# A language-model layer on one Trainium2 core: router logits of seven batches are taken during the next batch's attention, and the router's and first expert's inputs are loaded there

## The reference

```python
h = h + attention(layernorm(h))     # 8 heads of 128, rotary positions, causal softmax
h = h + experts(layernorm(h))
```

```python
scores = jax.nn.softmax(xt @ Wr, axis=-1)        # Wr is 256 by 8
G, idx = jax.lax.top_k(scores.T, k)              # each expert takes its 1024 best tokens
X_in = xt[idx]
h = jax.nn.gelu(jnp.einsum('ekd,edh->ekh', X_in, W1) + b1[:, None, :], approximate=False)
X_e = jnp.einsum('ekh,ehd->ekd', h, W2) + b2[:, None, :]
out = jnp.zeros((N, D)).at[idx.reshape(-1)].add((G[..., None] * X_e).reshape(E * k, D))
```

## Time and profile before

| what | value |
|---|---|
| median of 3 runs | 1323.09 us (1321.56 to 1324.31) |
| span of the profiled execution | 1321.1 us |
| TensorE busy | 1156.3 us, 88% of the span |
| DVE busy | 913.1 us, 69% |
| POOL busy | 746.2 us, 56% |
| ACT busy | 609.6 us, 46% |
| attention ends (start of the last `evacuate`, L402) | 774.27 us |
| first TensorE instruction of the experts' block | 807.52 us |
| first gathered rows on TensorE | 887.7 us |

### The profile page before, as it was taken

How to read it: one execution, slowest core, us unless ns; L and a number is a source line. 1 busy time by engine, 2 the same in 40 slices (tenths; PEclk the granted TensorE clock), 3 DMA queues, 4 the chain that set the end, 5 groups by cost and what they waited for, 6 DMA issues and landing times. The chain is left out here.

```text
span 1321.1 us, 22367 instructions
## 1 busy us (share of the span) xinstructions
PE 1156.3 (88%) x7255; PEld 990.9 (75%) x7255; DVE 913.1 (69%) x1980; ACT 609.6 (46%) x1306; POOL 746.2 (56%) x783
## 2 busy tenths in 40 slices
PE   2899999999999999999999983018999989898995
PEld 2688887878878878878888851017989879897995
DVE  4788888898898988888888844855545444454532
ACT  3454545545545555545455532005455445453542
POOL 2676676776776766766766610032473474644735
PEclk9999999999999999999999997559999999898998
DMA  5000100100100100101000003020351442423322
GB/s 179 1 17 1 37 30 0 40 24 0 40 24 27 33 4 32 32 0 36 28 1 32 17 32 105 0 97 17 96 126 23 110 113 30 114 36 92 54 29 33
DMA packets 42165, 57.51 MB, mean 44 GB/s; under 512 B 8896, under 2 KB 34944, under 8 KB 41984
## 3 DMA queue, kind: packets, MB, share of 16 engines
q0 software_dynamic: 13824, 21.24, 8.7%
q1 hardware_dynamic: 28288, 35.58, 8.0%
HBM read 35.71 MB, written 16.91 MB: 40 GB/s over the span
## 5 line engine op out<-in xcount | busy, mean ns | idle before, releaser
L1131 DVE TENSOR_TENSOR hT_lo<-hid,hT_hi 128x512 fp32r<-128x512 f32 x128 | 89.5, 702 | 160.9 <-ACT hT_hi L1245 160.9
L268 ACT ACTIVATE prob<-bank,row_min 128x512 f32<-128x512 f32 (+3 forms) x256 | 136.1, 532 | 112.6 <-DVE row_min L389 112.5
L199 POOL TENSOR_SCALAR prob<-prob,row_inv 128x512 f32<-128x512 f32 (+3 forms) x256 | 135.3, 540 | 68.3 <-DVE row_inv L393 66.8
L954 POOL DMA_INDIRECT got<-routed_rows,tokens x64 | 91.3, 1426 | 139.2 <-DVE tokens L1125 122.1
L1243 ACT ACTIVATE hid<-up,b_e 128x512 f32<-128x512 f32 x128 | 88.1, 688 | 161.3 <-PE up L1310 156.4
L339 DVE TENSOR_TENSOR pT_lo<-bank,pT_hi 128x384 fp32r<-128x384 f32 (+1 forms) x192 | 114.4, 596 | 50.5 <-ACT pT_hi L248 50.4
L212 POOL TENSOR_TENSOR kT_lo<-k_cos,kT_hi 128x512 fp32r<-128x512 f32 x64 | 82.6, 1290 | 77.7 <-ACT kT_hi L248 77.7
L248 ACT ACTIVATE oT_hi<-bank 128x512 fp32r<-128x512 f32 x64 | 38.3, 599 | 185.2 <-PE bank L519 177.3
L206 POOL TENSOR_TENSOR q_cos<-q_cos,q_sin 128x512 f32<-128x512 f32 x64 | 82.4, 1288 | 55.0 <-DVE q_sin L376 54.8
L974 POOL DMA_INDIRECT out<-y,tokens x64 | 103.0, 1609 | 17.3 <-issue 14.8
L389 DVE TENSOR_REDUCE row_min<-bank 128x1 f32<-128x512 f32 (+3 forms) x256 | 112.6, 481 | 0.2
(11 more groups left out here) (196 smaller groups left out, 3873.4 us busy)
## 6 DMA issues: line engine op xcount, KB each, us to landing
raw<-in_w SPq DMA_DIRECT2D x16, 1024.0 KB, 8.5
emb_res<-emb SPq DMA_DIRECT2D x8, 512.0 KB, 3.7
out<-h SPq DMA_DIRECT2D x8, 512.0 KB, 3.0
routed_rows<-x SPq DMA_DIRECT2D x8, 512.0 KB
x<-in_wq SPq DMA_DIRECT2D x1, 1024.0 KB, 7.5
x<-in_wk SPq DMA_DIRECT2D x1, 1024.0 KB, 11.2
x<-in_wv SPq DMA_DIRECT2D x1, 1024.0 KB, 5.3
x<-in_wo SPq DMA_DIRECT2D x1, 1024.0 KB, 8.5
```

What stands on the lines that cost most here:

```text
L199: nc.gpsimd.tensor_scalar(pr, pr, row_inv[:, h % 2, k:k + 1], 1.0, ALU.mult, ALU.mult).then_inc(s["norm_done"], 1)
L268: nc.scalar.activation(prob[:, h % 2, col:col + w], s_ps[bk][:, pc:pc + w], ACT.Exp, bias=row_min[:, h % 2, k:k + 1], scale=-1.0, accum_ou ...
L954: pool.indirect_dma_start(got[i][:, c, :], None, a["rows"][:, :], bass.IndirectOffsetOnAxis(tokens[i][:, c:c + 1], 0))\
L1131: nc.vector.tensor_tensor(out, in_, hi.bitcast(F32), ALU.subtract)\
```

## The change

- **Logits during attention.** `x2` shrinks to one batch (4 blocks), and a second buffer of that size, `x2T`, holds its transpose. In batches 1 to 7, for the batch before: at the end of slots 5 and 6 TensorE makes four transposes each into `proj_ps[1]` (`x2_turn`), ACT copies each to `x2T` (`x2_copy`), and at the end of slot 7 TensorE takes the logits token by expert into 32 columns of `proj_ps[1]` (`logits`: 8 float32 products, stationary `x2T` 128x128, moving `wr` 128x8), which ACT copies to `logit` (`keep_logits`). `project` of the key waits for these copies in slots 6, 7 and 0.
- **The router stage** handles the last batch alone: one group of 8 transposes, two copies, 8 products. The softmax of the first 28 blocks is taken in DVE's and ACT's gaps there, that of the last 4 at the end. The store of `score_rows` waits for the fourth signal of `r_score`, where it waited for the first.
- **Loads.** `groups_f` and `b1_rows` load at the kernel's start, behind `wr`; the first expert's `raw1` and `raw2` load in the last batch, ahead of the last store of `h2`.
- **What follows from the smaller `x2`.** Query, key and value weights pass through `raw1`, `raw2` and the `x2` pair, the output weight through `prob`, the mask through `k_cos`. `normalise2` waits for the last store of `x2` and its transposes.
- TensorE waits for `wr_in` ahead of its very first instruction, where it waited for it at the router's start. Batch 1 is written out as well; the loop covers batches 2 to 6.

```diff
@@ build_attention, SyncE
             sp.dma_start(wr[:], a["wr"].rearrange("(t p) e -> p t e", p=P))\
                 .then_inc(s["wr_in"], 16)
+            sp.dma_start(early["groups_f"][:], a["groups"][:, :, :]).then_inc(s["c_in"], 16)
+            sp.dma_start(early["b1_rows"][:], a["b1"].rearrange("e (t p) -> (e t) p", p=P))\
+                .then_inc(s["c_in"], 16)
...
             batches(sp, body)
+            sp.dma_start(early["raw1"][:], a["w1"][0].rearrange("(t p) n -> p t n", p=P))\
+                .then_inc(s["raw_in"], 16)
+            sp.dma_start(early["raw2"][:], a["w2"][0].rearrange("(t p) m -> p t m", p=P))\
+                .then_inc(s["raw_in"], 16)
             store_h2(B - 1)
@@ ScalarE
+            def x2_copy(b, kt):
+                after(act, "x2_tr", KT * b + kt + 1)
+                nc.scalar.activation(x2T[:, kt, :], proj_ps[1][:], ACT.Copy)\
+                    .then_inc(s["x2_copied"], 1)
+
+            def keep_logits(b):
+                after(act, "l_done", b + 1)
+                nc.scalar.activation(
+                    logit[:, bass.ds(b * TB, TB), :],
+                    l_ps.rearrange("p (t e) -> p t e", e=E), ACT.Copy).then_inc(s["l_kept"], 1)
...
                     if ok(h - 1):
                         exp(b, h - 1, 3)
+                    if h in (5, 6) and not (isinstance(b, int) and b == 0):
+                        x2_copy(b - 1, h - 5)
+                    if h == 7 and not (isinstance(b, int) and b == 0):
+                        keep_logits(b - 1)
@@ TensorE, project
                 if h == 0:
                     after(pe, "xt_lo", KT * (b + 1))
+                    if x == "k" and not (isinstance(b, int) and b < 2):
+                        after(pe, "l_kept", b - 1)
...
                     after(pe, "k_rope", n)
+                    if h in (6, 7) and not (isinstance(b, int) and b == 0):
+                        after(pe, "x2_copied", KT * (b - 1) + h - 5)
@@ TensorE
+            def x2_turn(b, kt, n):
+                after(pe, "x2_ready", TB * (b + 1))
+                after(pe, "k_rope", n + 1)
+                for tb in range(TB):
+                    last = nc.tensor.transpose(proj_ps[1][:, tb * P:(tb + 1) * P],
+                                               x2[:, tb, kt * P:(kt + 1) * P], ident[:])
+                last.then_inc(s["x2_tr"], 1)
+
+            def logits(b, live_xt):
+                after(pe, "x2_copied", KT * (b + 1))
+                if live_xt:
+                    after(pe, "xt_lo", KT * (b + 3))
+                for tb in range(TB):
+                    for kt in range(KT):
+                        last = nc.tensor.matmul(l_ps[:, tb * E:(tb + 1) * E],
+                                                x2T[:, kt, tb * P:(tb + 1) * P], wr[:, kt, :],
+                                                start=tb == 0 and kt == 0,
+                                                stop=tb == TB - 1 and kt == KT - 1)
+                last.then_inc(s["l_done"], 1)
+
             pe.wait_ge(s["tables_in"], 48)
+            pe.wait_ge(s["wr_in"], 16)
             xt(0)
```

More of the change, by code:

```diff
@@ L92, in build_attention @@
             out_done r_evac
-            stats2_done aggr2_done var2_eps rstd2_done apart""".split()
+            stats2_done aggr2_done var2_eps rstd2_done apart x2_tr x2_copied l_done l_kept""".split()
         s = {n: sem(n) for n in names} | shared
@@ L111, in batches @@
             body(0, range(8), lambda h: h >= 0)
-            with eng.Fori(1, B - 1) as b:
+            body(1, range(8), lambda h: True)
+            with eng.Fori(2, B - 1) as b:
                 body(b, range(8), lambda h: True)
@@ L658, in body @@
                         turn(b, h - 2, 2)
+                    if h in (5, 6) and not (isinstance(b, int) and b == 0):
+                        x2_turn(b - 1, h - 5, n)
+                    if h == 7 and not (isinstance(b, int) and b == 0):
+                        logits(b - 1, len(slots) == H)
             batches(pe, body)
@@ L738, in _ @@
             last.then_inc(s["r_aggr"], 1)
[L739 to L740 removed]
+            below_top(old, logit[:, old, :])
             dve.wait_ge(s["r_rstd"], 1)
+            dve.wait_ge(s["x2_out"], 16 * (B - 1))
             for tb in range(TB):
[L743 removed]
+                nc.vector.tensor_scalar(x2[:, tb, :], h2[:, tb, :], mean_var[:, tb, 0:1],
                                         rstd[:, tb:tb + 1], ALU.subtract, ALU.mult)\
@@ L815, in build_experts @@
-def build_experts(nc, a, ident, score, shared):
+            pe.wait_ge(s["x2_ready"], NB)
+            for kt in range(KT):
+                for tb in range(TB):
+                    last = nc.tensor.transpose(x_ps[kt][:, tb * P:(tb + 1) * P],
+                                               x2[:, tb, kt * P:(kt + 1) * P], ident[:])
+                last.then_inc(s["r_tr"], 1)
+            for kt in range(KT):
+                pe.wait_ge(s[f"r_copy{kt}"], 1)
+            for tb in range(TB):
+                for kt in range(KT):
+                    last = nc.tensor.matmul(l_ps[:, tb, :], x2T[:, kt, tb * P:(tb + 1) * P],
+                                            wr[:, kt, :], start=tb == 0 and kt == 0,
+                                            stop=tb == TB - 1 and kt == KT - 1)
@@ L817, in build_experts @@
+            last.then_inc(s["r_logits_done"], 1)
+def build_experts(nc, a, ident, score, early, shared):
     ctx = ExitStack()
@@ L823, in ps @@
             return ctx.enter_context(nc.psum_tensor(name, list(shape), F32))
-        groups_f, groups = sb("groups_f", [P, 2, P]), sb("groups", [P, 2, P], BF16)
+        groups_f, b1_rows, raw1, raw2 = (early[n] for n in ("groups_f", "b1_rows", "raw1", "raw2"))
+        groups = sb("groups", [P, 2, P], BF16)
         EH = 2
```

177 lines of the change are left out of this document (68 added, 109 removed).

## The result

The changed kernel takes 1330.11 us (median of 8 runs, 1322.88 to 1335.1), the kernel before 1322.74 us beside it (8 runs, 1319.85 to 1324.31). The ratio is 1.0069 with a 95% interval of 1.0045 to 1.0093: it is slower, by 0.69% or some 9 us (7.4 us between the two medians). I had forecast 1314.9 us and a range up to 1322.5. The profiled execution after has a span of 1327.1 us, 6.0 us more than before. So the sum of my steps, -8.2, misses +6.0 by 14 us, and the stages tell where. (The median lies near the 1330.9 us of my rival 2. That is chance: its mechanism, 4.1 us in every batch, isn't there.)

What follows compares the result with a forecast made beforehand. TensorE was taken to bound attention, with the router standing alone. Added 10.2 + 2.5 + 1.7 = 14.4 us, gained 18.7 + 3.9 = 22.6 us: -8.2 on the median 1323.1 gives 1314.9 us, range 1311.0 to 1322.5.

Steps and rivals of the forecast that it cites:

- rival 2: Attention, slots 5 to 7: the waits don't give way, 4.1 us in each of seven batches, 1330.9 us; chance 0.12.
- The price of the logits: Attention, TensorE: 16 loads with passes of 8 columns, starting 0.07 us apart, add 1.1 us a batch.
- my upper bound: Logits in attention: loads start 0.12 us apart, as 128-column fp32r loads do, 1.9 us a batch.
- That half clock: Router stage: TensorE, idle before it, does all its work there at granted clock 0.50, 1.2 GHz.
- Rival 1: Logits: loads start 0.12 us apart, as in fp32r, costing 7.2 us more, 1322.1 us, no measurable change; chance 0.25.
- the waits: Attention: TensorE's 3.0 us of lateness meets waits of 1.4 us in slot 7 and 0.8 us for `xT_lo`.
- DVE's lateness: Attention, from slot 6 on: DVE runs 0.6 us late, all that is left by the end of slot 7.
- the new waits: Attention: 1.5 us before `x2` is transposed after slot 5, and 0.2 to 0.3 us for ACT's copy.
- Batch 7: Last attention batch, without `xt`: one wait of 1.3 us absorbs its part, and 2.5 us are added.
- The router: Router stage: ends at 788.8 in place of 807.52, 18.7 us less, its last softmax taking 1.5 us.
- The tables: Start of the experts: DVE's wait of 3.93 us for the tables goes, 3.9 us gained.
- The start: Kernel start: the first transposes wait for `wr`, landing at 22.9, which adds 1.7 us.

Runs made afterwards that it cites:

- spread: Changed kernel with the eight logit products of batches 0 to 5 taken one by one between output-projection passes; 1315.3 us, ratio to before 0.9982.
- one_product: Changed kernel with only one of the eight logit products of a batch in attention; 1311.1 us, ratio to before 0.9950.
- tables_late: Changed kernel with the loads of `groups_f` and `b1_rows` back at the start of the expert stage; 1332.4 us, ratio to before 1.0096.
- before_far: Kernel before with 179 semaphore increments on DVE ahead of the search loop; 1335.0 us, one run.
- after_pad: Changed kernel with ten semaphore increments on DVE just ahead of the search loop; 1318.2 us, ratio to before 1.0041.
- before_pad: Kernel before with 19 semaphore increments on DVE ahead of the search loop; 1314.7 us, ratio to before 1.0020.
- no_idle: Changed kernel with ten DVE increments, `x2` transposes in later slots 1 and 2, logits in slot 7 ahead of `xt`; 1324.9 us, ratio to before 1.0051.
- spread_pad: spread with ten semaphore increments on DVE just ahead of the search loop; 1313.4 us, ratio to before 0.9966, and 0.9968 when run again.

## Why the prediction was wrong

**The price of the logits** is the term that was mis-sized. I gave 16 x 0.07 = 1.1 us, with L809 as the nearest row, and it is 16 x 0.118 = 1.9 us, my upper bound. L809's loads have 8 rows, and these have 128; the row that was like them in shape was the fp32r load that I kept for the bound. (L809 ran at full clock, so the clock is no part of the difference: its first row is at 784.7, and the window below has 1.00.) A batch without a fall grew by 2.2 us, not 1.7. In the router at half clock it is 3.55 us in place of 2.4. That half clock held as I took it, though my row was thin: the old stage was back at 1.00 after 780.4, and the new one is at 0.50. Rival 1 was right in its mechanism: it gave 1322.1 us, no change. By the Trainium skill's rule ("TensorE: Matmul & The Clock Gate", section "LDWEIGHTS (loading the stationary operand)"), a load of 128 columns takes 107 ns whatever its rows; for 128 rows the trace comes near it, at 118 ns from one to the next. The 0.07 us that I held against the rule are those of 8-row loads, which it doesn't fit, and which aren't what this change issues.

Windows of the kernel before and of the changed kernel in the router stage, columns as above:

```profile
780.40:807.50 27.10, 23.18 (x112) 9.82 (x111) 8.16 (x17) 8.70 (x15) 0.00 (x0) 1.00 0.06 19
```

```profile
806.70:810.20 3.50, 3.45 (x16) 3.48 (x16) 0.00 (x0) 0.00 (x0) 0.00 (x0) 0.50 0.02 5
```

**The clock in attention** is the step that was missing. I took half clock for the router, where TensorE stands still, and wrote that the logits "count in full", as if that were all they could do in attention. Behind them, in four batches of seven, everything ran at half clock for a while. This cost 4 x 1.6 = 6.4 us in the profiled run. That the eight products standing together bring it, spread (same passes, spread: none) and one_product (two passes: none) show, beside tables_late on the same chip (together: six falls).

**The search** was a term I didn't have: 3.1 us, because the change made DVE's program longer ahead of the loop by 179 instructions, by the unrolled second batch above all, and so moved the loop onto a bad place. before_far shows it on the old kernel.

**Right** were the waits. The 0.6 us for DVE's lateness are 2.2 - 1.9 = 0.3 in the trace (the wait for `xT_lo` didn't give way, the rest did), rival 2 (4.1 us a batch) fell, and the new waits stand where I put them: 1.3 us for 1.5 ahead of `x2`'s turning, and 0.2 for ACT's copy. Batch 7 without its fall is +2.5, as forecast, but by luck: its logits cost 0.8 us more than my term and the rest of it as much less. The router gives 17.4 for 18.7, the gap being the logits; its softmax took 811.79 - 810.34 = 1.45 us for 1.5. The tables give 3.8 for 3.9. **The start** cost 0.35 us for 1.7: `wr` landed at 21.57, earlier by 1.3 us than the 22.9 that I had from its issue at 14.72. In the changed kernel's profile it is issued at 13.6, and so it is in before_far, where the first transposes begin at 19.73. In after_pad they begin 1.7 us later than in before_pad on the same chip (21.34 and 19.67), so there the term holds, and the kernel before began late in the one profile that I had.

With the right price for the loads the forecast would have been -1, no change. The clock in attention (6.4), the search (3.1) and 1.6 us in the experts, where nothing was changed, make it 10.1. What came out smaller than my terms, 1.35 us at the start, 0.3 us a batch of DVE's lateness and 0.8 us in batch 7, takes it back to some 6.

The 1.6 us in the experts lie within what that stage differs by from one execution to another. Windows from the first gathered rows to the end, of the kernel before and of the changed kernel:

```profile
887.72:1321.10 433.38, 398.31 (x2656) 359.13 (x2656) 195.53 (x291) 206.23 (x303) 215.91 (x185) 0.95 0.32 68
```

```profile
892.16:1327.10 434.94, 399.96 (x2656) 360.50 (x2656) 194.43 (x291) 206.23 (x303) 214.36 (x185) 0.94 0.32 68
```

With the same work before_far took 427.7 us there at 0.96 and after_pad 424.6 us at 0.97: the stage is the shorter, the higher the granted clock.

## What to carry to other kernels

Work moved under a busy engine isn't free: here a batch grew by 2.2 us for 1.9 us of logits, and on top came what they did to the engine's clock. Look for stretches of loads with tiny passes, and spread them between long passes where they can't stand alone. Price a load by a row with the same number of rows and columns, since the pass behind it alone says nothing. When a tight loop gets slower without any change to it, compare the idle time at its end: a few instructions ahead of it can settle whether its place in the program is the cause.

## What the runs showed of the hardware that I had not expected

- The granted clock fell from 1.00 to 0.50 behind a stretch in which TensorE is hardly idle by the trace: 1.9 us of loads with passes of 8 columns stood ahead of it (no_idle, 388.8 to 391.0). It did not fall each time: behind the logits at 207.4 and 493.7 of the changed kernel it kept 1.00. Where it fell at 301.8 it was back by 305.5.
- A 20-instruction loop on DVE took 0.21 us more a round at one place of the program than at three others.
- A semaphore increment on DVE cost about 0.09 us ahead of the search (0.94 us for 10 in spread_pad, 1.8 for 19 in before_pad, 16.2 for 179 in before_far).
- The same kernel's runs differ by 4 to 16 us on a chip, and the longer ones have the lower mean granted clock: the changed kernel's eight runs go from 1322.88 us at 0.943 to 1335.1 us at 0.937.
